# Mamba block with int8 feed-forward: ScalarE clamps the growth exponent from PSUM, the running sum of delta goes, GpSimd adds five of sixteen terms

## The reference

```
A_bar = exp(d_c * A)                      # A = -exp(A_log), d_c = delta
BX = d_c * B_c * x_c
log_A_cum = cumsum(log(max(A_bar, 1e-10)))
A_cum = exp(min(log_A_cum, 80));  A_cum_sh = A_cum one position later
wcum = cumsum(BX / max(A_cum_sh, 1e-10))
h_chunk = A_cum * wcum / max(A_bar, 1e-10) + h * A_cum
y_c = sum over states of C * h_chunk  + D * x_c
```

## Time and profile before

| | us |
|---|---|
| median of 3 runs | 5842.17 (5839.98 to 5845.01) |
| span of the profiled execution | 5836.6 |
| PE busy | 5616.2 (96%) |
| DVE busy | 5351.4 (92%) |
| ACT busy | 3734.7 (64%) |
| POOL busy | 2457.2 (42%) |

### The profile page before, as it was taken

One profiled execution on the slowest core, in us unless ns is written; L12 is line 12 of the kernel. 1 busy time (PEld: TensorE's weight loads), 2 busy tenths in 40 slices (PEclk: granted clock), 3 DMA queues, 4 the chain that ended last, 5 costly groups with the idle time before them and its releaser, 6 DMA issues. The chain is left out here.

```text
span 5836.6 us, 78230 instructions
## 1 busy us (share of the span) xinstructions
PE 5616.2 (96%) x16088; PEld 2643.7 (45%) x16152; DVE 5351.4 (92%) x7057; ACT 3734.7 (64%) x4618; POOL 2457.2 (42%) x2139
## 2 busy tenths in 40 slices
PE   5999999999999999999999999999999999999998
PEld 2444444444444444444444444444444444444443
DVE  4999999999999999999999999999999999999997
ACT  3666666666666666666666666666666666666664
POOL 2444444444444444444444444444444444444443
PEclk9999999999999999999999999999999999999999
DMA  1122121121121211212212112112122121121220
GB/s 68 12 18 20 15 18 16 15 20 16 15 19 14 18 17 15 20 16 15 20 14 17 17 17 18 16 15 20 14 17 19 14 18 16 15 20 16 15 18 12
DMA packets 157893, 104.23 MB, mean 18 GB/s; under 512 B 121008, under 2 KB 121008, under 8 KB 157488
## 3 DMA queue, kind: packets, MB, share of 16 engines
q1 hardware_dynamic: 157488, 100.71, 19.0%
HBM read 42.63 MB, written 16.78 MB: 10 GB/s over the span
## 5 line engine op out<-in xcount | busy, mean ns | idle before, releaser
L487 POOL TENSOR_SCALAR room<-total,limit 128x1024 f32<-128x1024 f32 x1024 | 1183.1, 1155 | 3245.6 <-PE cum L1038 475.3
L739 ACT ACTIVATE decay<-cum,neg_a 128x1024 f32<-128x1024 f32 x1024 | 1137.3, 1111 | 1543.0 <-PE cum L1038 1539.3
L1048 PE MATMUL state<-sources,tri_upto 128*128 128x512 f32 x4096 | 1971.5, 604 | 123.9 <-DVE term L1380 123.5
L1038 PE MATMUL cum<-step,tri_before 128*128 128x512 f32 x4096 | 1938.8, 596 | 3.5 <-DVE sources L1367 3.5
L1380 DVE SCALAR_TENSOR_TENSOR term<-state,crow,decay 128x1024 f32<-128x1024 f32 x1024 | 1312.6, 1282 | 312.9 <-PE state L1048 196.0
L1390 DVE TENSOR_TENSOR acc<-acc,term 128x1024 f32<-128x1024 f32 x1024 | 1359.2, 1327 | 0.2
L1367 DVE SCALAR_TENSOR_TENSOR sources<-cum,brow,dx 128x1024 f32<-128x1024 f32 x1024 | 1305.5, 1275 | 10.0 <-ACT cum L755 10.0
L1038 PEld LDWEIGHTS cum<-step,tri_before 128*128 128x128 f32 x4096 | 781.1, 192 | 966.3 <-issue 943.7
L755 ACT ACTIVATE cum<-room,pos_a 128x1024 f32<-128x1024 f32 x1024 | 1143.6, 1117 | 110.6 <-POOL room L487 101.8
L1048 PEld LDWEIGHTS state<-sources,tri_upto 128*128 128x128 f32 x4096 | 743.3, 190 | 994.3 <-issue 867.3
L476 POOL TENSOR_SCALAR step<-delta,limit 128x1024 f32<-128x1024 f32 x1024 | 1144.7, 1118 | 8.3 <-PE cum L1038 7.0
(11 more groups left out here) (127 smaller groups left out, 3630.5 us busy)
## 6 DMA issues: line engine op xcount, KB each, us to landing
hfirst<-hrows SPq DMA_DIRECT2D x496, 64.0 KB, 3.9
xt<-in_x SPq DMA_DIRECT2D x64, 256.0 KB, 2.6
hrows<-term SPq DMA_DIRECT2D x1024, 4.0 KB, 1.6
xres<-in_x SPq DMA_DIRECT2D x64, 256.0 KB, 2.7
out_x<-xres SPq DMA_DIRECT2D x64, 256.0 KB, 2.1
gate_last<-gate SPq DMA_DIRECT2D x512, 0.5 KB, 2.0
win<-in_w_in SPq DMA_DIRECT2D x2, 2048.0 KB, 10.8
hrows<-hrows SPq DMA_DIRECT2D x64, 64.0 KB, 2.3
```

Of the source, the lines that this page charges most:

```text
L487: nc.gpsimd.tensor_scalar(room[:, :], total[:, :], limit[:, s:s + 1], 0.0, ALU.min, ALU.max).then_inc(limited, 1)
L739: nc.scalar.activation(decay[s % 4][:, :], cum[s % 2][:, :], ACT.Exp, scale=neg_a[:, s:s + 1]).then_inc(decay_ready, 1)
L1038: last = nc.tensor.matmul(cum[s % 2][:, cols], tri_before[:, :], step[s % 2][:, cols], start=True, stop=True)
L1048: last = nc.tensor.matmul(state[:, cols], tri_upto[:, :], source[s % 2][:, cols], start=True, stop=True)
```

## The change

`rooms` on ACT now makes `room` for every slot: it reads `cum` from PSUM, after `cum_ready`, and writes Relu(ln_top - a * cum) into `room`; `growths` then takes exp(ln_top - room). The choice between POOL and ACT (`ROOM_POOL`, `room_at`), POOL's `limit_sum`, the tile's sum `total` with PE's two matmuls, ACT's two copies and their semaphores are gone. The `add` of slots 0, 6, 7, 13 and 14 moves from DVE to POOL, where it stands behind `limit_step` of body `s+1`; the other eleven stay on DVE. In the waits, `norm_xnT` on PE now waits for `x2` of an earlier tile, which was covered by the wait for `total1`.

```
+GPSIMD_ADDS = (0, 6, 7, 13, 14)
...
-            def limit_sum(t, s):
...
-                nc.gpsimd.tensor_scalar(room[:, :], total[:, :], limit[:, s:s + 1], 0.0,
-                                        ALU.min, ALU.max).then_inc(limited, 1)
+            def add(t, s):
+
+                if s == 0:
+                    pool.wait_ge(front_pool, at(FRONT_POOL, t, "skip"))
+                else:
+                    pool.wait_ge(added, slot_at(t, s - 1))
+                pool.wait_ge(term_ready, slot_at(t, s))
                 stand(pool)
+                sums = acc[t.parity][:, :]
+                nc.gpsimd.tensor_tensor(sums, sums, term[s % 2][:, :], ALU.add).then_inc(added, 1)
...
                     if s + 3 < NS:
                         limit_step(t, s + 3)
                     elif more:
                         limit_step(nxt, s + 3 - NS)
+                    if s - 1 in GPSIMD_ADDS:
+                        add(t, s - 1)
...
             def rooms(t, s):
 
-                if s == min(x for x in range(NS) if x not in ROOM_POOL):
-                    act.wait_ge(front_act, at(FRONT_ACT, t, "total1"))
+                act.wait_ge(cum_ready, slot_at(t, s))
                 user, old = before(t, s, 1)
                 if user is not None:
                     act.wait_ge(growth_ready, slot_at(user, old))
-                nc.scalar.activation(room[:, :], total[:, :], ACT.Relu, bias=ln_top, scale=neg_a[:, s:s + 1]).then_inc(room_ready, 1)
+                nc.scalar.activation(room[:, :], cum[s % 2][:, :], ACT.Relu, bias=ln_top, scale=neg_a[:, s:s + 1]).then_inc(room_ready, 1)
...
                     if more or s + 2 < NS:
-                        if slot not in ROOM_POOL:
-                            rooms(ahead, slot)
+                        rooms(ahead, slot)
                         decays(ahead, slot)
...
-            def front_total(t, h):
...
-                nc.tensor.matmul((fbank, ebank)[h][:, :], tri_before[:, :], delta[t.parity][:, h * HALF:(h + 1) * HALF],
-                                 start=True, stop=True).then_inc(front_pe, 1)
...
-                    if s > 0:
+                    if s > 0 and s - 1 not in GPSIMD_ADDS:
                         add(t, s - 1)
-                    elif prev is not None:
+                    elif s == 0 and prev is not None:
                         add(prev, NS - 1)
```

More of the change, by code:

```diff
@@ L53 @@
 FRONT_ACT = ("xi0", "xi1", "xiT0", "tap3a", "xiT1", "tap3b", "z0", "xcT", "proj", "xc0", "abs", "exp", "over", "xc1",
-             "square", "ln", "z1", "total0", "total1", "ct")
-FRONT_PE = ("xi0", "xi1", "xiT0", "xiT1", "z0", "proj", "xc0", "xc1", "z1", "total0", "total1", "ct")
+             "square", "ln", "z1", "ct")
+FRONT_PE = ("xi0", "xi1", "xiT0", "xiT1", "z0", "proj", "xc0", "xc1", "z1", "ct")
 FRONT_POOL = ("skip",)
@@ L95, in slot_at @@
     return tile.n * NS + slot + 1
-def room_at(tile, slot):
-    same = [s for s in range(NS) if (s in ROOM_POOL) == (slot in ROOM_POOL)]
-    return tile.n * len(same) + same.index(slot) + 1
 def ring_at(tile, slot):
@@ L247, in mamba_block @@
         room_ready = sem("room_ready")
-        limited = sem("limited")
         cum_ready = sem("cum_ready")
@@ L526, in start @@
                     limit_step(t, s)
-                for s in range(2):
-                    if s in ROOM_POOL:
-                        limit_sum(t, s)
             def turn(t, s, more, more2):
@@ L556, in body @@
                     turn(t, s, more, more2)
[L557 to L560, removed]
                     if s + 3 < NS:
@@ L796, in start @@
                 for s in range(2):
-                    if s not in ROOM_POOL:
-                        rooms(t, s)
+                    rooms(t, s)
                     decays(t, s)
@@ L918, in norm_xnT @@
             def norm_xnT(t):
-                prev = t.shift(-1)
+                ended = t.shift(-3)
                 pe.wait_ge(norm_dve, at(NORM_DVE, t, "xn"))
-                if prev is not None:
-                    pe.wait_ge(front_act, at(FRONT_ACT, prev, "total1"))
+                if ended is not None:
+                    pe.wait_ge(end_dve, at(END_DVE, ended, "x2"))
                 turn4(lambda j: xn[:, j * P:(j + 1) * P], ebank).then_inc(norm_pe, 1)
@@ L955, in front_ct @@
                 nc.tensor.transpose(fbank[0:NS, P:2 * P], clast[:, :], ident[:, :]).then_inc(front_pe, 1)
-            def front_total(t, h):
-                earlier = t.shift(-2)
-                pe.wait_ge(front_dve, at(FRONT_DVE, t, "delta"))
-                if h == 0:
-                    front_free(t, "total0")
-                elif earlier is not None:
-                    pe.wait_ge(end_dve, at(END_DVE, earlier, "x2"))
-                nc.tensor.matmul((fbank, ebank)[h][:, :], tri_before[:, :], delta[t.parity][:, h * HALF:(h + 1) * HALF],
-                                 start=True, stop=True).then_inc(front_pe, 1)
             emptied = {"hT": (end_dve, END_DVE, "fixg"), "flag": (end_dve, END_DVE, "flag"), "yT0": (end_act, END_ACT, "yT0"),
@@ L1010, in end_attn, with end_qT @@
                     last.then_inc(end_pe, 1)
-            def end_qT(t, turned_in=None, summed_in=None):
+            def end_qT(t, turned_in=None):
                 if turned_in is not None:
                     pe.wait_ge(norm_act, at(NORM_ACT, turned_in, "xnT"))
-                if summed_in is not None:
-                    pe.wait_ge(front_act, at(FRONT_ACT, summed_in, "total1"))
                 pe.wait_ge(end_act, at(END_ACT, t, "q"))
@@ L1113, in body @@
                         if s == 0:
-                            end_qT(prev2, nxt if more else None, t)
+                            end_qT(prev2, nxt if more else None)
                         if s == 1:
@@ L1279, in front_delta @@
                     dve.wait_ge(step_ready, slot_at(earlier, NS - 1))
-                    dve.wait_ge(front_pe, at(FRONT_PE, earlier, "total1"))
                     dve.wait_ge(carry_logs, carry_at(earlier))
```

31 lines of the change are left out of this document (3 added, 28 removed).

## The result

The changed kernel takes 5978.57 us (median of 4 runs, 5975.68 to 5979.56), against 5842.2 us before: a ratio of 1.0232 with a 95% interval of 1.0218 to 1.0247, so 2.3% slower. 5969 us were forecast. The profiled execution spans 5977.8 us, 141.2 us more than before.

A forecast was written before the change was run, and what follows sets the result against it. A tile was taken as a chain: PE sets the pace in slots 7 to 11, DVE to 14, then PE. 5836.6 + 43 (ACT) + 74 (hold) + 10 (clock) = 5964 us span, 5969 us median; own range 5900 to 6020, 8-in-10 range 5800 to 6020.

The forecast's parts named there:

- The bound and PE's matmuls: Slots 11 to 14: DVE sets the pace, so removing PE's matmuls (1.72 us a tile) gains nothing; PE waits 2.2 us.
- the second rival: PE sets the pace throughout: its shorter list and two vanished waits shorten the run to 5690 us; chance 0.06.
- ACT's pass: Bodies 7 to 10: ACT's added PSUM pass delays its copy of `proj`, 0.7 us a tile, +43 us.
- The third rival: ACT becomes the bound in bodies 7 to 11, DVE waiting up to another 0.8 us a tile: 6020 us; chance 0.08.
- The hold: Around slots 14 and 15: POOL's add and `skip` hold DVE's small `end_refine` instructions, 1.2 us a tile, +74 us.
- What was put at nothing: Removing POOL's `room`, ACT's two copies of `total` and PE's two `delta` matmuls was counted as worth nothing.
- The sum: 5836.6 + 43 + 74 + 10 = 5964 us span, 5969 us median, 2.2% slower; chance of the forecast 0.58.
- The clock: Behind the 2.2 us wait before slot 14 PE's clock may fall, mostly absorbed before slot 15: +10 us, bounds 0 and 53.

The follow-up runs named there:

- The later `skip`: Kernel with no add on GpSimd, plus one unread 128x1024 pass on GpSimd in body 14 so that `skip` starts 1.1 us later: 5900.5 us.
- the kept matmuls: PE's two matmuls with `delta` put back in body 13, result unread: 5974.8 us in the changed kernel, 5856.6 us in that with no adds on GpSimd.
- add of 13 back: Changed kernel with the add of slot 13 back on VectorE, GpSimd keeping 0, 6, 7 and 14: 5890.3 us.
- `refine` alone: Changed kernel with the two small instructions of `refine` written with one tensor operand, columns given as scalars: 5815.3 us.
- both mends: Changed kernel with ACT's copy of `proj` ahead in body 8 and `refine` written with one tensor operand: 5806.3 us.
- late adds 2: Changed kernel with `proj` copy ahead, GpSimd adding slots 11, 12, 14 one body late, `skip` and DVE's `end_moments` in body 12: 5710.3 us.
- no adds, matmuls kept: Changed kernel with no adds on GpSimd and PE's two `delta` matmuls kept in body 13, result unread: 5856.6 us.

## Why the prediction was right, step by step

**The bound and PE's matmuls.** Right. The stretch from 11 to 14 stayed at 14.60 us without them; the wait before slot 14 became 2.01 us, 2.2 were forecast. Putting them back changed next to nothing in the changed kernel (5974.8), so the second rival is out. Its price was sound all the same: once work does leave DVE's list there, the stretch falls to 12.83 us, by 1.77 where 1.72 were counted.

**ACT's pass.** Right in place, 0.7 us forecast, 1.02 measured. The copy of `proj` is 0.67 of it, as worked out. The 0.07 us in body 7 was mis-sized: the pass takes 1.20 us and moves what follows by 1.10, not 1.01, and the product with `xcT` comes 0.28 us late. So +63 us instead of +43. The third rival came in a small part only: DVE waits 54.3 us in all for ACT's `cum`, 10.0 before.

**The hold.** Right: both instructions of `end_refine` end with POOL's add and `skip`, and `term` of slot 14 starts 5.14 us after its `states` (over 4.3 forecast), 0.86 us later than before (0.9 forecast). `xn` reads 1.71 us instead of 0.54, as allowed for. Taking the second tensor operand away took the hold of the small instructions away. What it cost per tile was right in one kind of tile only: a plain tile that is not slow reads 50.23 us with the hold and 49.04 with the adds of 13 and 14 back on DVE, 1.19 us, 1.2 forecast. But a slow plain tile reads 50.74 with it and 50.72 without. 20 of the 29 were slow without it, and so the mean over plain tiles rises by only 50.51 - 50.20 = 0.31 us, some 9 us in all. The turn tiles pay 54.46 - 51.03 = 3.43 us, some 99 us in all: there the delay comes on top of the turn's own wait, and `states` of slot 0 is slow in 16 of 28 turn tiles and in none without the hold. The term as a whole was too small, 74 us and 10 for the clock against 107.

The prediction took only a two-operand instruction on POOL to exclude such work on DVE. That was too narrow: POOL's `step`, with one tensor, holds DVE's add too (1.73 us, above).

The Trainium skill, "SBUF — State Buffer", section "SBUF: two separate sides", names two kinds of VectorE operation that take the shared ports against GpSimd: one with two SBUF inputs, and one in a two-port performance mode. The rows agree on the first: with two tensor operands 1.44 and 2.29 us, with one 0.26 and 0.21 us. `xn`, with one, is held as well; whether it ran in such a mode no run here shows.

**What was put at nothing.** Wrong for POOL's `room`, and in part for PE's matmuls. The removal of POOL's `room` was counted as worth nothing because it ended no wait of PE. It moved `skip`, and `skip` no longer held DVE's add of slot 13; without adds on POOL the turn reads 51.01 instead of 53.05 us. The later `skip` took 1.49 of these 2.04 us back, and the kept matmuls 0.72, so that without adds on POOL the removal of the matmuls has a part in the gain too. The five adds then spend it: `skip` stands behind the add of 13, and both hold `end_refine`.

**The sum.** The forecast was 43 + 74 + 10 = 127 us. Measured by the kernels between: the clamp from PSUM without `total` 33 us, the adds of 0, 6 and 7 nothing (-3), those of 13 and 14 107. By the table the 33 are 64 us of delay and some 22 of slow stretches in the plain tiles (0.73 in each), less some 61 gained at the turn (2.04 in each); this gives 25, and the profiled spans differ by 28. The mechanism is the one forecast, but that the total is right to 10 us is luck: the missed gain and the two undersized terms cancel.

**The clock.** Slow tiles behind slot 14 were forecast as a small term, and in the changed kernel it was: the kept matmuls remove them and save 50.51 - 50.23 = 0.28 us in a plain tile, 9 us, and 4 us in the medians. The reason given also held. With the wait before slot 15 a slow plain tile is 50.74 - 50.23 = 0.51 us longer than another; without that wait, with the adds of 13 and 14 back, it is 50.72 - 49.04 = 1.68.

## What to carry to other kernels

When work moves to GpSimd, list what VectorE runs beside it, down to the one-column instructions: the price is not the work but how long a small instruction with two tensors in SBUF stands, and where its result is awaited. Put GpSimd's passes beside VectorE's work that reads PSUM, and write column arithmetic with one tensor and scalars. A pass that leaves an engine moves what stood behind it; ask what that now collides with, or no longer does.

## What the runs showed of the hardware

- The granted clock does not follow from the length of one wait. Behind a wait of 2.01 us before slot 14 `states` ran slow in 1 of 57 tiles (add of 13 back), in 6 (`refine` alone), in 22 (after) and in 26 (both mends); with waits of 1.2 us and less in none. What decides between the tiles is open.
- POOL's TENSOR_SCALAR with one tensor also loses time against a DVE add (2.19 us for 1.12, late adds 2), though its row starts 0.06 us earlier. Where it starts 0.46 us earlier (no adds, matmuls kept) it is the add that is held, 1.73 us for 1.22.
- DVE's pass of `xn`, one tensor of 128x512 with two columns as scalars, is held (2.64 us for 0.54), while the same form on one column is not (0.26 us). Whether size or something else counts there, no run tells. By an estimate from these rows the wide pass takes (0.54 - 0.26) / 512 = 0.55 ns a column, while DVE's add takes 1.22 / 1024 = 1.2 ns, so it does not work at the add's pace.
